# Block-quantised weights prepared inside the first attention, and a low-rank term folded into the K and V weights

## The chip, the cores and the metric

The kernel runs on one core of one Trainium2 chip. The metric is the device time of one execution in microseconds (us). A core has five engines with a queue of instructions each: TensorE (PE in the profile, PEld for its weight loads), VectorE (DVE), ScalarE (ACT), GpSimd (POOL) and SyncE (SP, which here issues DMAs). They meet only at semaphores. The profile gives TensorE's granted clock as a share of 2.4 GHz: 1.00 is that, 0.50 is 1.2 GHz.

## The reference

Two layers over x of 4 x 1024 tokens by 256, with a context of 4 x 64 tokens by 192. Each layer is attention and then an MLP, both on a layer norm with a residual. The parts that the change touches are the weights of layer 0's MLP and the K and V of layer 1's attention:

```python
def lpbq_dequant(w):                       # w_gate, w_up: 768 x 256, w_down: 256 x 768
    O, I = w.shape
    qmax = 2.0 ** (W_BITS - 1) - 1.0       # W_BITS = 4, BLOCK = 32
    wb = w.reshape(O, I // BLOCK, BLOCK)
    s = jnp.maximum(jnp.max(jnp.abs(wb), axis=-1, keepdims=True) / qmax, 1e-12)
    wq = jnp.clip(jnp.round(wb / s), -qmax - 1.0, qmax) * s
    return wq.reshape(O, I)
...
x = act_qdq(x)                             # one scale over the whole normed x
up = act_qdq(x @ lpbq_dequant(w_up).T)
gate = act_qdq(x @ lpbq_dequant(w_gate).T)
sig = fixed_qdq_u16(jax.nn.sigmoid(gate))
gate = act_qdq(gate * sig)
o = act_qdq(gate * up)
return o @ lpbq_dequant(w_down).T
...
k_in = org_ctx @ Wk + _lora(org_ctx, k_down, k_up, k_alpha)   # rank 32, first 60 tokens
v_in = org_ctx @ Wv + _lora(org_ctx, v_down, v_up, v_alpha)
ipa_k = ipa_ctx @ Wk_ipa                                      # last 4 tokens
ipa_v = ipa_ctx @ Wv_ipa
```

## The kernel before

Everything lives in SBUF from stage to stage, and the stages follow one another as blocks: every engine waits at the end of a block until all have arrived. The 4096 tokens are 32 tiles of 128 (`NT`), tile t in `x_res[:, t, :]`. Matrices that TensorE multiplies are split in two f16 parts (`hi`, `lo`), which makes three products of each. The order of the work is written out by hand: each engine has its own loop, and there is no planner.

**Attention, layer 0** (`attention`, line 680). Each engine runs the same steps k over the tiles, with different tiles in flight, through `in_steps_by`: the first and last steps are written out, those between are a hardware loop of four steps (`Fori`). VectorE's step (line 961) is: `residual(k-2)`, `sums(k+1)`, `statistics(k-2)`, `inverses(k+1)`, `maxima(k+3)`, `rest_x(k+4)`, `rest_p(k)`. TensorE's is `scores(k+3)`, `turn_x(k+4)`, `turn_probs(k)`, `output(k-1)`. `scores(k+4)` needs what `rest_x(k+4)` writes. GpSimd's step is `normalise(k+1)`, which starts when `inverses(k+1)` has written `ri`, then `subtract(k+3)`, which needs `mx` of `maxima(k+3)`, then `add_bias(k+4)`; all three read and write SBUF (line 996 for the first two).

**Between attention and the MLP.** SyncE clears the semaphores (`clear_semaphores`, line 95). `quantise_weights` (line 1025) loads the three MLP weights (768 KB each) into `qw_w`, 128 x 1536 each; for each of them VectorE runs a chain in which every instruction waits for the one before: block maxima (L1068), their maximum (L1069), scale (L1070), its reciprocal (L1071), multiply (L1072), round (L1073), clip (L1074), multiply back (L1075). Then five small instructions make the powers of two `un` and `up` (L1077 to L1081), and the weights are turned on TensorE (L1117), four 128 x 128 blocks to a bank, nine banks, and split by ScalarE (`high`, L1095) and VectorE (`low`, L1086). `rstd_of` (line 642) turns the statistics into `rstd` and `nmr` (L652 to L666). `quantise_input` (line 1122) norms four tiles at a time (eight groups; ScalarE L1140), takes their largest value (L1159), turns them (L1151) and copies them into `xT` (L1164); it ends with the scale of the whole x. `gated_mlp` starts then: its first matmul (L1233) needs the scaled xT.

**gated_mlp** (line 1184) has three blocks. "gu" makes gate (16 units) and then up (16 units of 128 x 1536, `NU`), and SyncE stores up in HBM (L1395). "go" multiplies gate by up in 16 units: SyncE loads up again (L1426), ScalarE makes integer levels (L1506, L1508), VectorE multiplies and takes a maximum (L1520, L1514). Beside this, TensorE makes layer 1's K and V, 16 tiles of 128 x 256 (8 of K, 8 of V): SyncE loads the low-rank factors (`low_in`, eight DMAs), Wk and Wk_ipa, and, behind the third up load, Wv and Wv_ipa, into `xq`, which is free in this block. TensorE makes the two rank-32 products `cd` of the context (L1455), then for each tile two matmuls of Wk or Wv over 60 tokens of each batch (L1469, 128 and 64 rows), one of the low-rank factor (L1471, 32 rows) and two of the ipa weights over 4 tokens (L1474). ScalarE copies the tiles back (`keep`, L1488), one or two in each of the units 4 to 14 before the unit's own work; the six banks make a ring. "gd" is the down projection (from L1566).

The arena of 24576 floats per partition is taken after layer 0's attention: gate, xT, and later layer 1's `M` lie in it.

## Time and profile before

| | us |
|---|---|
| median of 3 runs (1607.9 to 1612.33) | 1609.33 |
| the profiled execution | 1618.78 |
| its span, first to last instruction | 1616.9 |
| PE busy / DVE busy / ACT busy / POOL busy | 1322.4 / 1037.8 / 809.5 / 518.5 |
| layer 0's attention, steady steps | 137 to 309 |
| last work of that attention to first matmul of the MLP | 326.4 to 395.7 |
| go, first K matmul to last copy | 572.5 to 642.3 |

An engine's busy time is the sum of its instructions' spans; a number after an arrow says what the engine had waited for. For this kernel the busy shares say little, since its stages have different limits: in attention TensorE has no gap, between attention and MLP VectorE works alone, and in go TensorE has no gap again, at half its clock.

### The profile page before, as it was taken

To read this page: it belongs to the slowest core of one execution; us is meant where nothing else is said; L and a number is where in the kernel's file an instruction comes from. 1 tells how busy PE (TensorE), PEld (TensorE's weight loads), DVE (VectorE), ACT (ScalarE), POOL (GpSimd) and SP (SyncE) were. 2 spreads that over 40 slices of the span, in tenths; PEclk is the share of its full clock that TensorE was granted. 3 is DMA by queue.
4 is the path that set the end of the run, shared out by engine and by line. 5 is a ranking of instruction groups with operands and counts; after the bars stand their busy time and mean duration, and the time that the engine had idled before them with its cause. 6 is when DMAs were issued, how large, how long until landed. Compare 5 with 4: busy or idle time off the path is not lost. (4 is left out here: it accounts for less than half of the span.)

```text
span 1616.9 us, 29377 instructions
## 1 busy us (share of the span) xinstructions
PE 1322.4 (82%) x8855; PEld 976.9 (60%) x8856; DVE 1037.8 (64%) x1908; ACT 809.5 (50%) x1173; POOL 518.5 (32%) x427
## 2 busy tenths in 40 slices
PE   5968999925997398598879999664099999999996
PEld 2435777713433145485546666564089989989995
DVE  2866777777569865464758888755255665666553
ACT  0345665505479665642567777564043344344341
POOL 1016777600000000001066767437513333333233
PEclk9979999957999755795899999855599999999998
DMA  5000000010013374200012122275422222222221
GB/s 199 1 3 1 1 0 0 1 59 1 0 66 148 143 235 169 106 8 1 11 46 93 63 90 65 59 276 173 151 54 45 47 49 40 46 47 51 40 44 12
DMA packets 63211, 106.86 MB, mean 66 GB/s; under 512 B 9712, under 2 KB 50768, under 8 KB 62000
## 3 DMA queue, kind: packets, MB, share of 16 engines
q1 hardware_dynamic: 48848, 89.17, 16.4%
q0 software_dynamic: 14304, 16.93, 5.7%
q8 instruction: 33, 0.54, 0.1%
q14 instruction: 26, 0.21, 0.0%
HBM read 67.89 MB, written 40.01 MB: 67 GB/s over the span
## 5 line engine op out<-in xcount | busy, mean ns | idle before, releaser
L2154 POOL DMA_INDIRECT out<-ex_yo,ex_mt x78 | 135.0, 1731 | 315.6 <-DVE ex_yo L2129 181.2
L2031 PE MATMUL ex_ps_h<-ex_xT_hi,a_arena 128*128 128x256 f16 x1248 | 211.8, 274 | 0.0
L2073 ACT ACTIVATE ex_hT<-ex_ps_h,e_b1T,e_unscale 128x256 f32<-128x256 f32 x312 | 150.5, 562 | 114.7 <-PE ex_ps_h L2031 114.7
L794 PE MATMUL at_ps_y<-c_VW,at_pT_hi 128*128 (+1 forms) x1024 | 171.9, 273 | 1.3 <-DVE main_x_res L921 1.3
L2031 PE MATMUL ex_ps_h<-ex_xT_lo,a_arena 128*128 128x256 f16 x624 | 170.7, 274 | 0.0
L2044 PE MATMUL ex_ps_y<-e_w_lo,ex_hT_hi 128*128 x624 | 170.2, 273 | 0.0
L2044 PE MATMUL ex_ps_y<-a_arena,ex_hT_lo 128*128 x624 | 170.2, 273 | 0.0
L2044 PE MATMUL ex_ps_y<-a_arena,ex_hT_hi 128*128 x624 | 170.2, 273 | 0.0
L996 POOL TENSOR_TENSOR at_sc<-at_sc,at_ri 128x960 f32<-128x960 f32 (+1 forms) x96 | 127.3, 1340 | 87.0 <-DVE at_ri L916 86.7
L1233 PE MATMUL gm_bank<-f_xq,f_wide 128*128 (+1 forms) x576 | 128.8, 384 | 21.2 <-ACT gm_stg L1271 16.2
L996 POOL TENSOR_TENSOR at_sc<-at_sc,at_mx 128x960 f32<-128x960 f32 (+1 forms) x96 | 127.2, 1339 | 43.1 <-DVE at_mx L893 42.9
L794 PE MATMUL at_ps_y<-c_VW,at_pT_lo 128*128 (+1 forms) x512 | 139.9, 273 | 0.0
L893 DVE TENSOR_REDUCE at_mx<-at_sc 128x16 f32<-128x960 f32 (+1 forms) x96 | 79.1, 852 | 92.3 <-ACT at_sc L829 92.3
L829 ACT COPY at_sc<-at_ps_s 128x1024 f32<-128x1024 f32 x64 | 64.7, 1011 | 134.6 <-PE at_ps_s L772 134.6
L2031 PEld LDWEIGHTS ex_ps_h<-ex_xT_hi,a_arena 128*128 x1248 | 122.5, 98 | 14.5 <-issue 0.3
L1233 PEld LDWEIGHTS gm_bank<-f_xq,f_wide 128*128 128x128 f16 x576 | 55.7, 99 | 94.2 <-issue 17.4
L2064 ACT ACTIVATE ex_xT_hi<-ex_ps_t 128x512 f16<-128x512 f32 x39 | 23.3, 597 | 176.2 <-PE ex_ps_t L2017 176.2
L794 PEld LDWEIGHTS at_ps_y<-c_VW,at_pT_hi 128*128 128x128 f16 x1024 | 100.3, 98 | 13.0 <-issue 1.8
L2105 DVE SCALAR_TENSOR_TENSOR ex_xT_lo<-ex_ps_t,ex_xT_hi 128x512 f16<-128x512 f32 x39 | 27.0, 691 | 113.8 <-ACT ex_xT_hi L2064 113.8
L2115 DVE TENSOR_TENSOR ex_hT_lo<-ex_hT,ex_hT_hi 128x1024 f16<-128x1024 f32 x78 | 95.7, 1227 | 2.7
L772 PE MATMUL at_ps_s<-a_arena,at_xnT_hi 128*128 (+1 forms) x256 | 79.7, 395 | 14.6 <-issue 10.9
L772 PE MATMUL at_ps_s<-c_M,at_xnT_hi 128*128 (+1 forms) x256 | 81.7, 403 | 10.3 <-issue 6.7
(320 smaller groups left out, 2941.7 us busy)
## 6 DMA issues: line engine op xcount, KB each, us to landing
at_half<-in_L_ffn_W SPq DMA_DIRECT2D x32, 512.0 KB, 4.0
up_scratch<-gm_stg SPq DMA_DIRECT2D x16, 768.0 KB, 3.2
gm_stg<-up_scratch SPq DMA_DIRECT2D x16, 768.0 KB, 4.2
ex_row<-xs SPq DMA_DIRECT2D x39, 260.0 KB, 2.7
rt_stage<-in_L_ffn_W SPq DMA_DIRECT2D x16, 512.0 KB, 6.2
main_x_res<-in_x SPq DMA_DIRECT2D x8, 512.0 KB, 12.0
out<-main_x_res SPq DMA_DIRECT2D x4, 1024.0 KB, 11.7
xs<-rt_pad SPq DMA_DIRECT2D x18, 130.0 KB, 2.2
```

Source lines behind the costliest of these rows:

```text
L772: last = nc.tensor.matmul(ps_s[j][:, c * CH:(c + 1) * CH], a[:, d, :], b[:, d, bass.ds(off + c * CH, CH)], start=(n == 0), stop=(n == 3 * ...
L794: last = nc.tensor.matmul(ps_y[:, 0:D], a[j][:, n, :], b[:, bass.ds(off + n * D, D)], start=(n == 0 and i == 0), stop=(n == NP - 1 and i = ...
L829: nc.scalar.copy(sc[j][:, :, :], ps_s[j % 2][:, :].rearrange("p (h k) -> p h k", h=H)).then_inc(ev_r, 1)
L893: last = nc.vector.tensor_reduce(mx[:, j, :, g], sc[j][:, :, lo:hi], AX.X, ALU.max)
L996: last = nc.gpsimd.tensor_tensor(part, part, what[:, j, :, g].unsqueeze(2).to_broadcast([P, H, hi - lo]), op)
L1233: last = nc.tensor.matmul(ps[:, o, :], a[:, d, o * P:(o + 1) * P], b[:, d, bass.ds(c0, CH)], start=(n == 0), stop=(n == 3 * DT - 1))
L2031: last = nc.tensor.matmul(ps_h[:, n, :], a[:, bass.ds(e * WN + d * HID + n * P, P)], b[:, d, :], start=(m == 0), stop=(m == 3 * DT - 1))
L2044: last = nc.tensor.matmul(ps_y[j][:, q, :], a[:, n, q * P:(q + 1) * P], b[:, bass.ds(e * WN + n * D, D)], start=(n == 0 and m == 0), stop= ...
L2073: last = nc.scalar.activation(hT[:, n, :], ps_h[:, n, :], ACT.Relu, bias=b1T[:, bass.ds(e * HT + n, 1)], scale=unscale[:, 0, bass.ds(e, 1)])
L2105: nc.vector.scalar_tensor_tensor(out=xT_lo[j][:, :, :], in0=ps_t[:, :, :], scalar=XN_SCALE, in1=xT_hi[j][:, :, :], op0=ALU.mult, op1=ALU.s ...
L2115: nc.vector.tensor_tensor(hT_lo[j][:, part, :], hT[:, part, :], hT_hi[j][:, part, :], ALU.subtract).then_inc(hlo_r, 1)
L2154: nc.gpsimd.indirect_dma_start(out=acc[:, :], out_offset=bass.IndirectOffsetOnAxis(ap=mt[j][:, q, 1:2].bitcast(U32), axis=0), in_=yo[j][:, ...
```

## The change

Two edits that don't touch each other.

**First edit: the MLP weights.** `quantise_weights` and the `rstd_of` ahead of the MLP are gone. The arena is taken before layer 0's attention, whose `M`, projection weights and `WqT` now lie in it, and so do the three MLP weights. SyncE issues their loads at the start of attention. VectorE does the chain in 12 steps of attention (k = 4 to 15), four for each weight, between `inverses` and `maxima`; for this its loop is written out in full instead of `Fori`. The maximum over partitions is one GpSimd instruction at the end, and the powers follow VectorE's last step. The turning and splitting of the nine banks, and the work of `rstd_of`, go into `quantise_input`.

**Second edit: layer 1's K and V.** The rank-32 up factor is loaded as rows 64 to 95 of the second half of Wk or Wv, and `cd` is put under the context's second half in `ctxe`, so that the low-rank matmul joins the 64-row one (now 96 rows). The down factors are padded with 64 zero columns by GpSimd so that `cd` comes out in rows 64 to 95. The small loads are issued in gu behind its first store, Wk's loads at gu's end, Wv's at go's start; ScalarE does its part of `cd` ahead of unit 0 instead of in units 1 and 2.

```diff
@@ attention, VectorE
+            def levels(i, part):
+                wi, per, am, sc, rs = qw[i], [P, NB, QB], bam[:, i, :], bsc[:, i, :], brs[:, i, :]
+                if part == 0:
+                    dve.wait_ge(loaded[i], 16)
+                    nc.vector.tensor_reduce(am, wi, AX.X, ALU.max, apply_absolute_value=True).then_inc(qc, 1)
+                elif part == 1:
+                    dve.wait_ge(qc, 7 * i + 1)
+                    nc.vector.tensor_reduce(top[:, i:i + 1], am, AX.X, ALU.max).then_inc(top_r, 1)
+                    nc.vector.tensor_scalar(sc, am, 1.0 / 7.0, 1e-12, ALU.mult, ALU.max).then_inc(qc, 1)
...
+                    nc.vector.reciprocal(rs, sc).then_inc(qc, 1)
...
+                    nc.vector.tensor_tensor(wi, wi, rs.unsqueeze(2).to_broadcast(per), ALU.mult).then_inc(qc, 1)
+                elif part == 2:
...
+                    nc.vector.tensor_scalar(wi, wi, MAGIC, MAGIC, ALU.add, ALU.subtract).then_inc(qc, 1)
...
+                    nc.vector.tensor_scalar(wi, wi, 7.0, -8.0, ALU.min, ALU.max).then_inc(qc, 1)
+                else:
...
+                    nc.vector.tensor_tensor(wi, wi, sc.unsqueeze(2).to_broadcast(per), ALU.mult).then_inc(qc, 1)
...
                 if there(k + 1, NT):
                     inverses(k + 1, (j + 1) % NS)
+                if quant and 4 <= k < 16:
+                    levels((k - 4) // 4, (k - 4) % 4)
                 if there(k + 3, NT):
                     maxima(k + 3, (j + 3) % NS)
...
-            in_steps_by(nc.vector, NT, 4, 2, NS, step)
+            if quant:
+                for k in range(-4, NT + 2):
+                    step(k, k % NS)
+                powers()
+            else:
+                in_steps_by(nc.vector, NT, 4, 2, NS, step)
@@ quantise_input, ScalarE
+            high(0)
+            high(1)
+            act.wait_ge(ve_r, 1)
+            nc.scalar.activation(sd[:, :], ve[:, :], ACT.Sqrt).then_inc(sd_r, 1)
+            high(2)
+            act.wait_ge(nmr_r, 1)
+            for g in range(NC):
+                norm(g)
+                if g + 3 < NM:
+                    high(g + 3)
@@ gated_mlp, gu, SyncE
                     sp.dma_start(up_dram[u, :, :], stg[u % 2][:, :]).then_inc(u_st[u % 2], 16)
+                    if u == 0:
+                        sp.wait_ge(u_mm, 1)
+                        for i, n in enumerate("kv"):
+                            split(sp, downs[:, i, :, C1:UP], l1[f"{n}_down"], low_in)
+                            sp.dma_start(alpha[:, i:i + 1], l1[f"{n}_alpha"].unsqueeze(0).to_broadcast([P, 1])
+                                         ).then_inc(low_in, 16)
+                load_kv(sp, 0)
@@ gated_mlp, go, TensorE
-                        for t in range(2):
-                            nc.tensor.matmul(tokens(out, 0, KV - IPA), wt[0:rows[t], t, at],
-                                             tokens(ctxT[0:rows[t], t, :], 0, KV - IPA), start=(t == 0), stop=False)
-                        nc.tensor.matmul(tokens(out, 0, KV - IPA), ups[i][:, at], tokens(cd[i], 0, KV - IPA),
+                        nc.tensor.matmul(tokens(out, 0, KV - IPA), wt[:, 0, at], tokens(ctxT[:, 0, :], 0, KV - IPA),
+                                         start=True, stop=False)
+                        nc.tensor.matmul(tokens(out, 0, KV - IPA), wt[0:UP, 1, at], tokens(ctxe[0:UP, i, :], 0, KV - IPA),
                                          start=False, stop=True)
```

Where the instructions stand. VectorE in layer 0's attention, one step of the loop before, from `sums` on (`at_sm` are the sums, `at_ri` the inverses, `at_mx` the maxima, `at_xnT_lo` what the next scores wait for; the REGISTER and ISA rows are the loop's addresses):

```order
L911 TENSOR_REDUCE at_sm<-at_sc 128x16
L926 ISA
L926 BN_STATS main_stats<-main_x_res 128x6
L916 RECIPROCAL at_ri<-at_sm 128x16
L893 TENSOR_REDUCE at_mx<-at_sc 128x16
L897 REGISTER_ALU
L898 SCALAR_TENSOR_TENSOR at_xnT_lo<-at_ps_xT,at_xnT_hi 128x256
```

and the same place in the changed kernel, in step 5 (the second quarter of the first weight; `at_bam`, `at_bsc`, `at_brs` are block maxima, scales and reciprocals, `a_arena` here the weight):

```order
L847 TENSOR_REDUCE at_sm<-at_sc 128x16
L862 BN_STATS main_stats<-main_x_res 128x6
L852 RECIPROCAL at_ri<-at_sm 128x16
L905 TENSOR_REDUCE at_top<-at_bam 128x1
L906 TENSOR_SCALAR at_bsc<-at_bam 128x48
L908 RECIPROCAL at_brs<-at_bsc 128x48
L910 TENSOR_TENSOR a_arena<-a_arena,at_brs 128x1536
L829 TENSOR_REDUCE at_mx<-at_sc 128x16
L834 SCALAR_TENSOR_TENSOR at_xnT_lo<-at_ps_xT,at_xnT_hi 128x256
```

Four instructions of the weights now stand between the inverses and the maxima, ahead of everything that the next scores wait for; in step 4 it is one (L902), in step 6 two (L913, L915), in step 7 one (L918), and then again for the next weight.

VectorE in the changed kernel at the start of `quantise_input` (`f_wide` receives the low parts of the gate and up weights, `qx_xn` is a group of normed tiles, `qx_ps` the turned one):

```order
L1112 BN_AGGR main_mv<-main_stats 128x2 x32
L1115 TENSOR_SCALAR qx_ve<-main_mv 128x32
L1099 SCALAR_TENSOR_TENSOR f_wide<-qx_ring,a_up,f_wide 128x2x256 x2
L1119 RECIPROCAL main_rstd<-qx_sd 128x32
L1121 SCALAR_TENSOR_TENSOR main_nmr<-main_mv,main_rstd 128x32
L1099 SCALAR_TENSOR_TENSOR f_wide<-qx_ring,a_up,f_wide 128x2x256
L1104 TENSOR_REDUCE qx_am<-qx_xn 128x1
L1099 SCALAR_TENSOR_TENSOR f_wide<-qx_ring,a_up,f_wide 128x2x256
L1104 TENSOR_REDUCE qx_am<-qx_xn 128x1
L1109 COPY a_arena<-qx_ps 128x2x512
```

Before, the nine low parts were all done ahead of the statistics; now three stand ahead of the first group and six among the groups.

TensorE at the start of go, before (`f_xq` holds Wk or Wv and the ipa weights, `f_wide` the low-rank operands):

```order
L1455 MATMUL gm_bank<-main_ctxT,f_wide 32x4x60 x4
L1469 MATMUL gm_bank<-main_ctxT,f_xq 128x4x60 x2
L1471 MATMUL gm_bank<-f_wide 128x4x60
L1474 MATMUL gm_bank<-main_ctxT,f_xq 128x4x4 x2
L1469 MATMUL gm_bank<-main_ctxT,f_xq 128x4x60 x2
```

and now:

```order
L1430 MATMUL gm_bank<-main_ctxT,f_wide 96x4x60 x4
L1441 MATMUL gm_bank<-main_ctxT,f_xq 128x4x60
L1443 MATMUL gm_bank<-f_wide,f_xq 128x4x60
L1446 MATMUL gm_bank<-main_ctxT,f_xq 128x4x4 x2
L1441 MATMUL gm_bank<-main_ctxT,f_xq 128x4x60
```

A tile has four matmuls instead of five: the one over `f_wide` alone is gone, and the second one over the weights reads its moving side from `f_wide`.

## Rows read from the trace of the kernel before

**Rows 1.** By stretch: length, busy PE, PEld, DVE, ACT, POOL, then PEclk, DMA, GB/s.

```profile
137.00:326.00 189.00, 187.08 (x1394) 140.17 (x1392) 142.21 (x239) 109.25 (x172) 128.61 (x85) 1.00 0.00 0
572.00:642.00 70.00, 69.53 (x160) 39.70 (x160) 42.92 (x26) 40.38 (x39) 0.00 (x0) 0.50 0.53 180
835.00:1035.00 200.00, 188.31 (x1364) 138.11 (x1363) 165.35 (x346) 155.67 (x249) 139.42 (x146) 0.99 0.25 77
```

**Rows 2.** Timeline of DVE, one attention step: start, length, what; idle before it.

```profile
216.44 0.48 DVE L921 SCALAR_TENSOR_TENSOR main_x_res<-at_ps_y,c_unscale,main_x_res 128x256 f32 x1
...
218.31 0.23 DVE L916 RECIPROCAL at_ri<-at_sm 128x16 f32<-128x16 f32 x1
220.04 1.22 DVE L893 TENSOR_REDUCE at_mx<-at_sc 128x16 f32<-128x1024 f32 x1 [1.50 <-ACT at_sc L829]
221.18 0.41 DVE L898 SCALAR_TENSOR_TENSOR at_xnT_lo<-at_ps_xT,at_xnT_hi 128x256 f16<-128x256 f32 x1
...
222.75 0.48 DVE L921 SCALAR_TENSOR_TENSOR main_x_res<-at_ps_y,c_unscale,main_x_res 128x256 f32 x1
```

**Rows 3.** Timeline of POOL in the same step.

```profile
218.62 1.90 POOL L996 TENSOR_TENSOR at_sc<-at_sc,at_ri 128x1024 f32<-128x1024 f32 x1 [0.99 <-DVE at_ri L916]
```

**Rows 4.** Timeline of PE in the same step: the scores that need at_xnT_lo.

```profile
222.43 0.59 PE L772 MATMUL at_ps_s<-c_M,at_xnT_hi 128*128 x2
```

**Rows 5.** Timeline from the end of attention to the first MLP matmul.

```profile
325.98 0.43 DVE L926 BATCH_NORM_STATS2 main_stats<-main_x_res 128x6 f32<-128x256 f32 x1
...
329.94 0.38 SPq L1052 DMA_DIRECT2D qw_w<-in_L_ffn_w_gate  x1
...
334.78 1.75 DVE L1068 TENSOR_REDUCE qw_am<-qw_w 128x48 f32<-128x1536 f32 x1 [8.38 <-DMA qw_w<-in_L_ffn_w_gate]
336.57 0.20 DVE L1069 TENSOR_REDUCE qw_top<-qw_am 128x1 f32<-128x48 f32 x1
...
339.18 0.96 DVE L1073 TENSOR_SCALAR qw_w<-qw_w 128x1536 f32<-128x1536 f32 x1
...
341.17 1.76 DVE L1075 TENSOR_TENSOR qw_w<-qw_w,qw_sc 128x1536 f32<-128x1536 f32 x1
...
358.96 0.16 DVE L1077 TENSOR_SCALAR qw_gtop<-qw_gtop 128x3 f32<-128x3 f32 x1
...
360.62 4.29 DVE L1086 SCALAR_TENSOR_TENSOR f_wide<-qw_ring,qw_up,f_wide 128x512 f16<-128x512 f32 x6 [0.81 <-ACT f_wide L1095]
...
367.75 1.28 ACT L666 ACT_TABLE_LOAD   x1 [1.07 <-PEq L78]
367.78 2.21 DVE L652 BATCH_NORM_AGGREGATE main_mv<-main_stats 128x2 f32<-128x6 f32 x32 [0.32 <-PEq L78]
...
371.37 8.18 ACT L1140 ACTIVATE qx_xn<-main_x_res,main_nmr,main_rstd 128x256 f32<-128x256 f32 x16 [0.89 <-PEq L78]
...
395.72 4.62 PE L1233 MATMUL gm_bank<-f_xq,f_wide 128*128 128x512 f16 x11 [4.99 <-DVE f_xq L1312]
```

**Rows 6.** Timeline at the start of layer 1's preparation: two instructions side by side.

```profile
737.01 3.51 POOL L446 MEMSET a_arena<- 128x4096 f32 x1 [82.20 <-POOLq L97]
...
737.05 3.49 DVE L514 TENSOR_SCALAR pa_alpha_r<-a_arena 128x2 f32<-128x2 f32 x1 [4.86 <-PEq L97]
```

**Rows 7.** Timeline of go: first matmuls, one K tile, and the last copy.

```profile
559.06 1.57 ACT L1506 ACTIVATE gm_gq<-a_arena,gm_sc 128x1536 int16<-128x1536 f32 x1 [8.65 <-PEq L78]
...
567.49 3.81 PE L1455 MATMUL gm_bank<-main_ctxT,f_wide 128*32 128x240 f32 x8 [26.79 <-DMA f_wide<-in_L_xattn_v_up]
...
572.47 2.26 PE L1469 MATMUL gm_bank<-main_ctxT,f_xq 128*128 128x240 f32 x4 [1.16 <-DMA f_xq<-in_L_xattn_Wk_ipa]
...
574.66 1.16 PE L1471 MATMUL gm_bank<-f_wide 32*128 32x240 f32 x2
...
576.83 2.26 PE L1469 MATMUL gm_bank<-main_ctxT,f_xq 128*128 128x240 f32 x4
...
642.34 0.37 ACT L1488 COPY f_xq<-gm_bank 128x256 f32<-128x256 f32 x1 [3.99 <-PE gm_bank L1474]
```

More of the change, by code:

```diff
@@ L278, in _ @@
                 last.then_inc(made, 1)
-            for base, ipa in ((wk, wki if lora else None), (wv, wvi if lora else None)):
-                if base is wv and not lora:
+            for base in (wk, wv):
+                if base is wv:
                     pe.wait_ge(late, 16 * len(second))
@@ L1122, in quantise_input @@
[L1122 to L1135 removed]
+                nc.scalar.activation(hi, banked(m), ACT.Copy, scale=up[:, i:i + 1]).then_inc(high_r, 1)
@@ L1136, in _, with norm @@
+            def norm(g):
                 need(act, t_r, g - 1)
@@ L1142, in _, with turn_w, turn_x @@
                 last.then_inc(xn_r, 1)
+            high(0)
[8 more added lines that the diff above has]
+                    high(g + 3)
+            for m in range(NC + 3, NM):
+                high(m)
         @block.tensor
         def _(pe):
-            for g in range(NC):
+            def turn_w(m):
+                i, g = divmod(m, 3)
+                src = w[i].rearrange("p (o b) q -> p o (b q)", o=DT if i == 2 else FT)
+                need(pe, moved, m - 3)
+                for a in range(2):
+                    for b in range(2):
+                        if i < 2:
+                            blk = src[:, 2 * g + b, a * P:(a + 1) * P]
+                        else:
+                            blk = src[:, b, (2 * g + a) * P:(2 * g + a + 1) * P]
+                        last = nc.tensor.transpose(ring[:, m % 4, (2 * a + b) * P:(2 * a + b + 1) * P], blk, ident[:, :])
+                last.then_inc(made, 1)
+            def turn_x(g):
                 pe.wait_ge(xn_r, g + 1)
@@ L1387, in _ @@
                 nc.gpsimd.partition_all_reduce(allr[:, 0:1], red[:, 0:1], P, RMAX).then_inc(gall, 1)
+                pool.wait_ge(u_mm, 1)
+                nc.gpsimd.memset(downs[:, :, :, 0:C1], 0.0).then_inc(low_set, 1)
+                for i in range(2):
+                    nc.gpsimd.tensor_copy(ctxe[0:C1, i, :], ctxT[0:C1, 1, :]).then_inc(low_set, 1)
                 pool.wait_ge(gred, 2)
```

355 lines of the change are left out of this document (133 added, 222 removed).

## The prediction

> **What bounds the kernel now.** I read three views in this order. The busy time by stretch tells which engine has no gap: in layer 0's attention TensorE is busy for 187.1 of 189 us at granted clock 1.00 while VectorE has 142.2, and in go's stretch with the K and V tiles TensorE is busy for 69.5 of 70 us at 0.50 while VectorE has 42.9 and ScalarE 40.4 [rows 1]. The timeline of one attention step then shows where VectorE's spare time lies: a step is 222.75 - 216.44 = 6.31 us, and its one wait, 1.50 us, is between the inverses (done at 218.54) and the maxima at 220.04 [rows 2]. Last, the timeline between attention and MLP shows a chain on VectorE with TensorE idle: from the last statistics, 326.41, to the first MLP matmul, 395.72, 69.3 us pass [rows 5]. So the first edit moves work from a stretch in which nothing hides it into a gap of an engine that isn't the bound, and the second takes a matmul from the bound of its stretch.
>
> **First edit, what goes.** After it the stretch from 326.41 on is made of these. The clearing of the semaphores and the block change stay, 329.94 - 326.41 = 3.5 us [rows 5]; six semaphores more are cleared here and six fewer at the next clearing, so that cancels. The five small powers now end attention: 358.96 to 359.81 (the low at 360.62 less its idle of 0.81), so 0.85 us, exposed as before [rows 5]. Until the first normed tile, ScalarE does two highs (some 0.8 us each, by the idle of 0.81 ahead of the first low), the table load of 1.28 and the root; the statistics of 2.21 us run beside this on VectorE. With about 1.1 us for the first turned bank that is 4.0 us, and 371.37 - 369.99 = 1.4 us lie between statistics and first norm as before, with part of a third high 5.9 us [rows 5]. From the first norm to the first MLP matmul it was 395.72 - 371.37 = 24.35 us, set by VectorE with its maximum and copy for each group; six lows at 4.29 / 6 = 0.715 us now stand among them, 4.3 us, and ScalarE's highs stay under VectorE's time: 28.6 us [rows 5]. The sum is 3.5 + 0.85 + 5.9 + 28.6 = 38.9 us, against 69.3: **30.4 us less**. The loads of the weights (waited for until 334.78) and both chains' block changes are gone with this; the loads run under attention, whose DMA share is 0.00 [rows 1].
>
> **First edit, what attention pays.** The chain costs, by start to start, 1.79 us in its first quarter, 339.18 - 336.57 = 2.61 in its second, 341.17 - 339.18 = 1.99 in its third and 1.76 in its last [rows 5]. It stands in the gap of 1.50, so the maxima start later by 0.29, 1.11, 0.49 and 0.26, that is 2.15 us for a weight and 6.5 for three. VectorE is the bound for these 12 steps, and queued behind each piece are the maxima and at_xnT_lo, for which TensorE's scores wait; they start 222.43 - 221.59 = 0.84 us after it [rows 2, 4], a slack that is used up once: 5.6 us. That is the lower end.
>
> But the gap is not empty on the neighbour: GpSimd's normalise starts at 218.62, right behind the inverses, and lasts to 220.52 [rows 3]. In this trace a tensor_scalar from SBUF to SBUF of two elements a partition took 3.49 us, and ended with the GpSimd memset of 3.51 us that had started 0.04 us before it [rows 6]. I take it that such an instruction waits for the GpSimd one that is running, and the other way round. In the second quarter L906 (the tensor_scalar) comes behind the small L905, so behind normalise's start: it is held until 220.52, and 2.4 us are then left, so the maxima start at 222.9, 2.9 us late. In the third the first tensor_scalar is ahead of normalise (VectorE's next instruction starts 0.08 us before its last one ends), normalise goes between the two (1.90), and the second comes behind: 0.99 + 1.90 + 1.0 from 218.46 on, 2.3 us late. The first quarter is a reduce and the last one starts ahead: 0.29 and 0.26. Together 5.75 for a weight, 17.3 for three, less the slack: **16.4 us more**, the value I take, since the held instruction is of the same kind. If normalise gets ahead in the last quarter too, that adds 1.9 three times: 22 us, the upper end. GpSimd's delay of some 2 us costs nothing, as the probabilities are wanted a whole step later.
>
> The Trainium skill (SBUF — State Buffer, Who interferes with whom) states this as a rule: VectorE and GpSimd share one pair of ports, held for a whole instruction by whichever starts first, and both tensor_scalar from SBUF and an instruction with two SBUF inputs need it, a reduce does not. The memset row agrees for the tensor_scalar. No row here shows the two-input case held. By the rule the sum is the 16.4 us above; by the plain durations it would be 5.6 us.
>
> **Second edit.** A K tile took 576.83 - 572.47 = 4.36 us, and its two wide matmuls 2.19, so 1.09 each [rows 7]. The low-rank one, of the same width, goes: 3.27 us. The 96-row matmul is taken at the price of the 64-row one, since those of 128 and 64 rows are in the same 2.19; the clock stays at 0.50, as in the whole stretch [rows 1]. TensorE stood waiting for the small loads until 567.49 though the block had begun at 559.06; it can start at once now, since the small loads come in gu and Wk's behind gu's last store, under VectorE's tail. The start until the first tile, 572.47 - 567.49 = 5.0 us, gets 0.3 for the wider products: first tile at 564.4, last one done at 564.4 + 16 x 3.27 = 616.7, where it was 642.3 [rows 7]: 25.5 us less. ScalarE starts its unit 0 some 5 us later, which doesn't show as long as a unit takes less than (616.7 - 564.4) / 14 = 3.7 us; the 42.9 and 40.4 us of VectorE and ScalarE in that stretch [rows 1] fit in 52.3. What follows the last copy stays. In gu, GpSimd's padding and copies (three instructions of at most 256 elements a partition, each between 0 and the 1.9 us of a 1024-element one [rows 3]) may hold VectorE: 0.5 us. Six small DMA issues ahead of gu's second store have a whole unit of time. **25.0 us less.**
>
> **Sum.** -30.4 + 16.4 - 25.0 = -39.0 us. The profiled execution of 1618.78 us would become 1579.8; it is 9.4 us above the median of the runs shown, 1609.33, and the terms don't depend on that, so the median becomes **1570.3 us**.
>
> **The rivals.** (1) No holding by GpSimd: attention pays 5.6 us, the sum is -49.8, 1559.5 us. For it: no row shows VectorE's large instructions held. Against it: the 3.49 us of two elements. (2) Normalise gets ahead in every quarter but the first: 22 us, the sum is -33.4, 1576. (3) In go the units, not the tiles, set the end: it decides from 3.7 us a unit; at the 4.36 us of today's tiles the last unit is some 9 us later, 1579. Against it are the busy times. (4) In go TensorE gets the full clock, since its work is denser without the low-rank matmul: the units set the end some 5 us earlier, 1565. Against it: the stretch was gapless and stayed at 0.50. (5) Slower: the gaps of up to 2.9 us that VectorE now makes in TensorE's work let the granted clock fall to 0.50 in the 12 steps. A step of 6.31 us of gapless work then takes another 6.31, 75.7 us in all, against the 30.4 + 25.0 = 55.4 that the edits bring: +20 us, 1629.6; it decides from 55.4 / 6.31 = 8.8 steps at the lower clock. Against it: layer 1's attention leaves TensorE idle for 11.7 of 200 us with a clock of 0.99 [rows 1].
>
> **How the numbers follow.** Forecast 0.56, rival 1 0.20, rival 2 0.08, rival 3 0.05, rival 4 0.04, rival 5 0.04, and 0.03 that terms fail together and leave it where it is. Both signs: 0.93 is faster by over 0.3% (4.8 us, about what runs of this kernel tell apart), 0.03 within it, 0.04 slower. The range reaches from rival 1 with 3 us for the spread of the runs to rival 3: 1556 to 1581.
>
> **What would show it.** After the last statistics the first MLP matmul comes about 39 us later. In attention the steps k = 4 to 15 come in fours: near 6.5, 9.2, 8.6 and 6.5 us if GpSimd holds, 6.6, 7.4, 6.8, 6.6 if not; L906 then lasts near 2 us instead of 0.2, and the second tensor_scalar of the third quarter near 2.9 instead of 0.96. The granted clock there stays at 1.00. In go the K tiles start within 6 us of the block at 3.27 us each. The prediction is wrong if the small pieces in attention push the scores by more than their own length plus one normalise, or if ScalarE waits for up loads rather than for tiles in go.

## The result and the profile after

The changed kernel takes **1561.33 us** (median of 3 runs, 1559.65 to 1561.85) where the kernel before took 1609.33. The ratio is 0.970, with a 95% interval of 0.967 to 0.972, so 48.0 us less. The prediction was 1570.3 us with a range of 1556 to 1581: right in sign and range, 9 us too high.

The profiled execution took 1561.33 us, with a span of 1559.6. Against the profiled one of before, 1618.78, it is 57.4 us less, and that is 9.4 us more than the medians differ. Points at which the work passes from stage to stage, from both timelines, tell where the difference lies:

| stage | before | after | change | predicted |
|---|---|---|---|---|
| start to the first turned tile of attention 0 | 103.3 | 91.1 | -12.2 | 0 |
| attention 0: first turned tile to the start of the last statistics | 222.7 | 233.4 | +10.7 | +16.4 |
| from there to the first MLP matmul | 69.7 | 38.4 | -31.3 | -30.4 |
| MLP, first to last matmul of gu | 144.6 | 144.9 | +0.3 | +0.5 |
| last matmul of gu to first of gd | 126.1 | 97.2 | -28.9 | -25.5 |
| all that follows, to the end of the span | 950.5 | 954.6 | +4.1 | 0 |

The first row is no effect of the change, as experiment 1 shows.

By stretch (length, busy PE, PEld, DVE, ACT, POOL, then PEclk, DMA, GB/s), which answers to [rows 1]. The first is layer 0's attention: TensorE now has 12.5 us of idle time, at the full clock, and VectorE is busy for 20 us more. The second is go, at the lower clock.

```profile
137.00:326.00 189.00, 176.53 (x1305) 131.33 (x1303) 161.84 (x254) 101.83 (x160) 126.05 (x80) 1.00 0.00 0
...
526.00:596.00 70.00, 47.24 (x136) 39.11 (x136) 54.98 (x40) 53.85 (x52) 0.35 (x1) 0.50 0.70 234
```

**The stretch behind attention** is as predicted. One timeline of all engines (start, length, engine, line, what, count, and in brackets the idle time before it), which answers to [rows 5]:

```profile
324.53 0.43 DVE L862 BATCH_NORM_STATS2 main_stats<-main_x_res 128x6 f32<-128x256 f32 x1
...
325.54 0.17 DVE L932 TENSOR_SCALAR a_up<-a_up 128x3 f32<-128x3 f32 x1
...
329.76 2.22 DVE L1112 BATCH_NORM_AGGREGATE main_mv<-main_stats 128x2 f32<-128x6 f32 x32 [4.05 <-PEq L97]
...
334.62 2.08 ACT L1046 ACTIVATE qx_xn<-main_x_res,main_nmr,main_rstd 128x256 f32<-128x256 f32 x4
...
362.88 1.46 PE L1217 MATMUL gm_bank<-f_xq,f_wide 128*128 128x512 f16 x3 [4.55 <-DVE f_xq L1296]
```

The reader is to see four steps from the end of the statistics at 324.96: the powers until 325.71, clearing and block change until 329.76, until the first norm 334.62 - 329.76 = 4.9 us, and from it to the first matmul 362.88 - 334.62 = 28.3 us.

**Attention** pays. The timelines of DVE and of POOL, which answer to [rows 2, 3]; a "piece" is one of the four parts of a weight's chain. First a step with the second piece, then one with the third and one with the last. The rows of L857 are the residuals, so from one to the next is a step:

```profile
176.57 0.48 DVE L857 SCALAR_TENSOR_TENSOR main_x_res<-at_ps_y,c_unscale,main_x_res 128x256 f32<-128x256 f32 x1
...
178.64 0.18 DVE L906 TENSOR_SCALAR at_bsc<-at_bam 128x48 f32<-128x48 f32 x1
178.85 0.45 DVE L908 RECIPROCAL at_brs<-at_bsc 128x48 f32<-128x48 f32 x1
179.34 2.92 DVE L910 TENSOR_TENSOR a_arena<-a_arena,at_brs 128x1536 f32<-128x1536 f32 x1
182.19 1.21 DVE L829 TENSOR_REDUCE at_mx<-at_sc 128x16 f32<-128x1024 f32 x1
...
184.84 0.47 DVE L857 SCALAR_TENSOR_TENSOR main_x_res<-at_ps_y,c_unscale,main_x_res 128x256 f32<-128x256 f32 x1
```

```profile
178.75 1.90 POOL L976 TENSOR_TENSOR at_sc<-at_sc,at_ri 128x1024 f32<-128x1024 f32 x1 [0.94 <-DVE at_ri L852]
```

```profile
156.02 0.47 DVE L857 SCALAR_TENSOR_TENSOR main_x_res<-at_ps_y,c_unscale,main_x_res 128x256 f32<-128x256 f32 x1
...
158.02 0.90 DVE L913 TENSOR_SCALAR a_arena<-a_arena 128x1536 f32<-128x1536 f32 x1
158.95 2.53 DVE L915 TENSOR_SCALAR a_arena<-a_arena 128x1536 f32<-128x1536 f32 x1
...
164.06 0.47 DVE L857 SCALAR_TENSOR_TENSOR main_x_res<-at_ps_y,c_unscale,main_x_res 128x256 f32<-128x256 f32 x1
...
166.06 1.69 DVE L918 TENSOR_TENSOR a_arena<-a_arena,at_bsc 128x1536 f32<-128x1536 f32 x1
...
170.32 0.48 DVE L857 SCALAR_TENSOR_TENSOR main_x_res<-at_ps_y,c_unscale,main_x_res 128x256 f32<-128x256 f32 x1
```

```profile
158.18 2.49 POOL L976 TENSOR_TENSOR at_sc<-at_sc,at_ri 128x1024 f32<-128x1024 f32 x1 [0.94 <-DVE at_ri L852]
...
166.22 3.29 POOL L976 TENSOR_TENSOR at_sc<-at_sc,at_ri 128x1024 f32<-128x1024 f32 x1 [0.94 <-DVE at_ri L852]
...
172.49 1.90 POOL L976 TENSOR_TENSOR at_sc<-at_sc,at_ri 128x1024 f32<-128x1024 f32 x1 [0.43 <-DVE at_ri L852]
```

The rows read as if whoever starts first kept the other waiting, and experiment 3 tests that. The product L910 started 0.59 us after GpSimd's normalise and took 2.92 us, where the same instruction took 1.76 in the kernel before with GpSimd idle. It ends 1.6 us after normalise, which ends at 180.65. In the third piece L913 was ahead, normalise (2.49 us for 1.90) waited for its end, and L915 (2.53 us for 0.96) waited for normalise. In the last piece the product was ahead and took its plain length, and normalise stretched to 3.29. At 172.49 VectorE runs the first piece, a reduce of 1.70 us over 1536 elements, and normalise keeps its 1.90. The steps of the first, second, third and last piece took 6.25, 8.27, 8.04 and 6.26 us, where a step without a piece takes 6.31.

**go**, which answers to [rows 7], in the timelines of PE, ACT and DVE:

```profile
526.65 4.21 PE L1430 MATMUL gm_bank<-main_ctxT,f_wide 128*96 128x240 f32 x8 [18.52 <-PEq L78]
...
531.40 1.17 PE L1441 MATMUL gm_bank<-main_ctxT,f_xq 128*128 128x240 f32 x2 [0.54 <-ACT f_wide L1454]
532.37 1.01 PE L1443 MATMUL gm_bank<-f_wide,f_xq 96*128 96x240 f32 x2
533.16 0.98 PE L1446 MATMUL gm_bank<-main_ctxT,f_xq 128*128 128x16 f32 x4
534.08 1.17 PE L1441 MATMUL gm_bank<-main_ctxT,f_xq 128*128 128x240 f32 x2
...
574.63 0.98 PE L1446 MATMUL gm_bank<-main_ctxT,f_xq 128*128 128x16 f32 x4
```

```profile
542.74 1.58 ACT L1479 ACTIVATE gm_sq<-gm_stg,gm_sc 128x1536 int16<-128x1536 f32 x1 [3.91 <-DMA gm_stg<-up_scratch]
...
580.33 0.69 ACT L1460 COPY f_xq<-gm_bank 128x256 f32<-128x256 f32 x2
```

```profile
544.42 1.76 DVE L1491 TENSOR_TENSOR a_arena<-gm_gq,gm_sq 128x1536 f32<-128x1536 int16 x1 [3.53 <-ACT gm_sq L1479]
546.09 1.75 DVE L1485 TENSOR_REDUCE gm_pmax<-a_arena 128x1 f32<-128x1536 f32 x1
547.75 1.75 DVE L1491 TENSOR_TENSOR a_arena<-gm_gq,gm_sq 128x1536 f32<-128x1536 int16 x1
...
592.80 0.17 DVE L1496 TENSOR_REDUCE gm_red<-gm_pmax 128x1 f32<-128x16 f32 x1
```

The first tile starts 4.9 us after the block, and a tile takes 534.08 - 531.40 = 2.68 us, not 3.27. The tiles end at 575.6, 17.2 us before the unit work does at 592.80. In the kernel before that distance was 11.9 us, from 642.3 to this row of its DVE timeline:

```profile
654.19 0.17 DVE L1525 TENSOR_REDUCE gm_red<-gm_pmax 128x1 f32<-128x16 f32 x1
```

From 544.42 on VectorE has no gap, at 547.75 - 544.42 = 3.33 us a unit. So the units and not the tiles set the end, and they were held by a load, 3.91 us ahead of 542.74. The prediction had named just this, ScalarE waiting for up loads rather than for tiles, as a sign that it is wrong.

### The profile page after: what moved, and what is told of

The parts are those of the page before. It is cut to its first block and busy times, and to the rows that moved or that the text cites. A ratio compares the mean times of both kernels' runs of the same rounds, so it can differ in the third digit from the quotient of the medians.

```text
span 1559.6 us, 29136 instructions
## 1 busy us (share of the span) xinstructions
PE 1280.5 (82%) x8823; PEld 967.2 (62%) x8824; DVE 1042.2 (67%) x1908; ACT 809.1 (52%) x1173; POOL 522.7 (34%) x430
## 3 DMA queue, kind: packets, MB, share of 16 engines
q1 hardware_dynamic: 48848, 89.17, 17.2%
## 5 line engine op out<-in xcount | busy, mean ns | idle before, releaser
L708 PE MATMUL at_ps_s<-a_arena,at_xnT_hi 128*128 (+1 forms) x512 | 162.8, 401 | 34.0 <-issue 26.7
L976 POOL TENSOR_TENSOR at_sc<-at_sc,at_ri 128x960 f32<-128x960 f32 (+1 forms) x96 | 133.4, 1403 | 83.5 <-DVE at_ri L852 83.2
L708 PEld LDWEIGHTS at_ps_s<-a_arena,at_xnT_hi 128*128 128x128 f16 x512 | 51.3, 101 | 93.4 <-issue 48.9
L730 PEld LDWEIGHTS at_ps_y<-c_VW,at_pT_hi 128*128 128x128 f16 x1024 | 100.0, 98 | 12.7 <-issue 1.8
L708 PE MATMUL at_ps_s<-a_arena,at_xnT_lo 128*128 (+1 forms) x256 | 102.1, 399 | 0.0
## 6 DMA issues: line engine op xcount, KB each, us to landing
main_x_res<-in_x SPq DMA_DIRECT2D x8, 512.0 KB, 11.9
```

Of the source, the lines that this page charges most:

```text
L708: last = nc.tensor.matmul(ps_s[j][:, c * CH:(c + 1) * CH], a[:, d, :], b[:, d, bass.ds(off + c * CH, CH)], start=(n == 0), stop=(n == 3 * ...
L730: last = nc.tensor.matmul(ps_y[:, 0:D], a[j][:, n, :], b[:, bass.ds(off + n * D, D)], start=(n == 0 and i == 0), stop=(n == NP - 1 and i = ...
L976: last = nc.gpsimd.tensor_tensor(part, part, what[:, j, :, g].unsqueeze(2).to_broadcast([P, H, hi - lo]), op)
```

## The experiments

All runs were timed against the kernel before on their own chip, and chips differ: its median was 1622.4 us in the first set, 1605.9 in the second and 1623.9 in the third. Most of that lies in layer 1's MLP, which sends every token to some of several expert weights: from the last tile turned for the choice of experts (the route) to the first one turned for the experts' products 45.9 to 47.8 us pass in the profiles of the first measurement and of the second set, and 53.7 to 58.9 in those of the first and third set, whatever the kernel. So kernels of different sets are compared by stages, from the timelines (attention 0 from the first turned tile to the start of the last statistics, then to the first MLP matmul, then from gu's last matmul to gd's first):

| kernel | set | median | attention 0 | to first MLP matmul | gu's last to gd's first |
|---|---|---|---|---|---|
| token axis flat | 1 | 1623.9 | 220.0 | 69.8 | 126.3 |
| second edit alone | 1 | 1589.7 | 222.9 | 69.8 | 96.6 |
| first edit alone | 1 | 1602.5 | 233.3 | 38.4 | 127.1 |
| pieces ahead of inverses | 1 | 1563.0 | 225.4 | 38.4 | 96.7 |
| changed kernel | 2 | 1561.6 | 233.5 | 38.3 | 96.9 |
| units 2, 3 ahead of Wv | 2 | 1560.4 | 233.1 | 38.4 | 97.9 |
| loads not early | 2 | 1569.5 | 232.5 | 38.4 | 108.1 |
| 27 pieces, units ahead | 2 | 1548.9 | 222.4 | 38.3 | 98.6 |
| changed kernel | 3 | 1575.9 | 233.2 | 38.4 | 97.0 |
| Wv loaded in gu | 3 | 1572.7 | 232.9 | 38.4 | 94.0 |
| third product | 3 | 1586.8 | 233.4 | 38.3 | 112.9 |
| 27 pieces, Wv in gu | 3 | 1561.7 | 222.1 | 38.4 | 95.6 |

The 220.0 in the first line, where the kernel before has 222.7, is no cheaper step: the steps take the same time as before, and the difference lies ahead of the first residual.

**1. The 12.2 us ahead of attention.** The diff also writes layer 0's K and V projections with a flat token axis, and the prediction had no term for that. The edit, made in the kernel before:

```diff
-                            last = nc.tensor.matmul(
-                                ring[:, b, 0:B * KV].rearrange("p (b k) -> p b k", b=B)[:, :, lo:hi],
-                                wt[0:m, t, j * P:(j + 1) * P],
-                                ctxT[0:m, t, :].rearrange("p (b k) -> p b k", b=B)[:, :, lo:hi],
-                                start=(t == 0), stop=(t == 1))
+                            last = nc.tensor.matmul(ring[:, b, 0:B * KV], wt[0:m, t, j * P:(j + 1) * P], ctxT[0:m, t, :],
+                                                    start=(t == 0), stop=(t == 1))
```

> The kernel before with one edit: the K and V projections of layer 0 write and read their 256 tokens as one flat axis and not as 4 groups of 64 (the diff changes this on the side, and my prediction has no term for it). In the profiles the 64 matmul records of these projections stand 0.575 us apart before and 0.314 after the change, and the first score-matrix product starts at 59.84 and 47.26 us. Theory A, the access pattern is the cause: the projections take 0.31 us a record here too, the stage ends some 12.6 us earlier, and the median is 1609.3 - 12.6 = 1596.7 us. Theory B, the profiled execution of the kernel before ran its projections at the lower clock by chance (it was 9.4 us above its median): the median stays within 3 us of 1609.3.

Its time over that of before is 1.002 (0.998 to 1.006): no gain. The matmuls of Wk in the timelines of PE, in the kernel before and in the kernel with the second edit alone, which keeps the old axis:

```profile
22.18 18.31 PE L288 MATMUL pa_ring<-main_ctxT,pa_wk 128*128 128x256 f32 x32
```

```profile
22.52 10.01 PE L288 MATMUL pa_ring<-main_ctxT,pa_wk 128*128 128x256 f32 x32
```

The same code took 18.3 us once and 10.0 us once. The first score-matrix product came at 59.8 us in that one profile and between 46.5 and 48.6 in the thirteen others. Only one of the thirteen, the second edit alone, has the old token axis; that the axis brings nothing is shown by the medians above.

The clock tells what happened in that execution. In go at clock 0.50 the median weight load takes 310 ns, and so it does here, where the kernel with the second edit alone shows 186. The row of the clock prints 1.00 for the stretch, but the trace of before holds no record of the clock ahead of 65.4 us, and a stretch without one prints as 1.00. The timeline of PEld shows the change at that record, within one run of equal weight loads:

```profile
65.12 0.34 PEld L298 LDWEIGHTS pa_ring<-pa_Kd,pa_WqT 128*128 128x128 f32 x1 [0.52 <-issue]
65.72 0.19 PEld L298 LDWEIGHTS pa_ring<-pa_Kd,pa_WqT 128*128 128x128 f32 x1 [0.26 <-issue]
```

In the thirteen other traces the first record of the clock stands between 21.5 and 25.1 us, and the weight loads shorten there too. So theory B holds with its mechanism: TensorE ran this stage at the lower clock until 65.4 us, some 40 us longer than in the others, after the same start. Its 1618.78 us are 9.4 above the median of that kernel, and the late stage is 12.2. Why the clock rose late that once is open. Without the 12.2 us the profiled pair differs by 45.1 us, and the medians by 48.0 (and by 1605.9 - 1561.6 = 44.3 in the second set).

**2. Each edit alone.** The gated MLP of one kernel put into the other.

> The kernel before with the second edit alone (the low-rank product folded into 96 rows, small loads and Wk's in gu). My prediction's term is -25.0, which gives 1584.3 us; the profile of the changed kernel, read from the last gated matmul to the first down matmul, gives -28.9, which gives 1580.4. In either case layer 0's attention and the 69 us after it are as in the kernel before. If the edits only bring their sum together, this and the first edit alone add up to -48.0.

> The changed kernel with the gated MLP of the kernel before, so the first edit alone (with the flat token axis). My prediction's terms are -30.4 + 16.4 = -14.0, which gives 1595.3 us. The profile of the changed kernel gives -31.4 for the stretch after attention and +10.7 for attention, -20.7, which gives 1588.6; if the flat token axis brings 12.6 in every execution and not in the profiled one alone, it is 1576.

The ratios to before are 0.980 (0.975 to 0.984) and 0.987 (0.982 to 0.991), by the medians -32.7 and -19.9 us, together -52.6 against -48.0; on this chip the runs of before spread over 23 us, so the stages tell more. Each edit acts in its own stages: go's way is shorter with the second alone (96.6 us, against 97.2 with both), and attention is longer and the stretch behind it shorter with the first alone (233.3 and 38.4, against 233.4 and 38.4). The edits add up.

**3. Is it GpSimd that makes the pieces long?** VectorE's step, with `levels` moved:

```diff
+                if quant and 4 <= k < 16:
+                    levels((k - 4) // 4, (k - 4) % 4)
                 if there(k + 1, NT):
                     inverses(k + 1, (j + 1) % NS)
-                if quant and 4 <= k < 16:
-                    levels((k - 4) // 4, (k - 4) % 4)
```

> The changed kernel with each piece of the weights' chain put ahead of the inverses, where GpSimd waits for VectorE and nothing of it runs. Theory A, the pieces cost more than their length because GpSimd's normalise runs beside them (2.92 us for the first product where 1.76 is its length, 2.53 for the second tensor_scalar where 0.90 is): none is held here, the steps with the second and third piece go from 8.27 and 8.04 us to about 7.1 and 6.35, which is 2.9 us for a weight and 8 us for three: 1561.3 - 8 = 1553 us. Theory B, VectorE reads its operands more slowly in these forms whatever GpSimd does: the durations stay at 2.9 and 2.5 us and the time at 1561. Rival C, normalise now starts up to 2.5 us later and the subtract behind it too, so the exponentials come late and the gain is given back: the time is 1558 or more though the durations fall.

The timelines of DVE and of POOL there:

```profile
147.90 0.47 DVE L857 SCALAR_TENSOR_TENSOR main_x_res<-at_ps_y,c_unscale,main_x_res 128x256 f32<-128x256 f32 x1
...
150.55 1.76 DVE L910 TENSOR_TENSOR a_arena<-a_arena,at_brs 128x1536 f32<-128x1536 f32 x1
152.22 0.25 DVE L852 RECIPROCAL at_ri<-at_sm 128x16 f32<-128x16 f32 x1
...
154.99 0.47 DVE L857 SCALAR_TENSOR_TENSOR main_x_res<-at_ps_y,c_unscale,main_x_res 128x256 f32<-128x256 f32 x1
...
156.84 0.98 DVE L913 TENSOR_SCALAR a_arena<-a_arena 128x1536 f32<-128x1536 f32 x1
157.85 0.96 DVE L915 TENSOR_SCALAR a_arena<-a_arena 128x1536 f32<-128x1536 f32 x1
...
161.49 0.47 DVE L857 SCALAR_TENSOR_TENSOR main_x_res<-at_ps_y,c_unscale,main_x_res 128x256 f32<-128x256 f32 x1
```

```profile
152.55 1.90 POOL L976 TENSOR_TENSOR at_sc<-at_sc,at_ri 128x1024 f32<-128x1024 f32 x1 [2.75 <-DVE at_ri L852]
```

Theory A. No operand and no shape was changed, only GpSimd's product no longer stands beside them, and L910 falls from 2.92 to 1.76 us, L915 from 2.53 to 0.96. Attention takes 225.4 us, 8.0 less, as expected. The steps with the second and third piece take 154.99 - 147.90 = 7.09 and 161.49 - 154.99 = 6.50 us. That is what VectorE's own work of 4.55 us (6.25 less the reduce of 1.70) and the pieces' 2.5 and 2.0 us add up to, so the later normalise cost nothing and rival C falls. The time by itself can't show the 8 us: the median of 1563.0 us is from the first set, in which the changed kernel did not run. Its ratio to before, 0.962 (0.958 to 0.967), lies below the changed kernel's 0.970 to 0.973.

The Trainium skill (SBUF — State Buffer, Who interferes with whom) states this as an exclusive lock that whoever starts first holds for its whole instruction. By it a VectorE instruction with two SBUF inputs needs the lock against a GpSimd one that reads SBUF, a tensor_scalar needs it in its 2-port mode, and a reduce never does. The three cases here, 2.92 us, 2.53 us and the reduce beside a normalise of 1.90, agree.

**4. The changed kernel again**, for the second and third set.

> The changed kernel itself once more, on the same chip as the other runs of this set, so that they can be compared with it. The time is 1561 us where the kernel before has 1609; on another chip both may be later by the same amount. Layer 0's preparation is expected as in the first profile of the changed kernel (first score-matrix product near 47.3 us), since two of three kernels with the old token axis had it there too.

> The changed kernel on the chip of this set, as the one to compare with: 1561 us where the kernel before has 1606 to 1609.

1561.6 and 1575.9 us, with ratios to before of 0.973 (0.970 to 0.976) and 0.972 (0.967 to 0.976), as in the first measurement.

**5. The early start alone and the fold alone.** Without the early loads: six small loads out of gu's queue and Wk's too, all issued in go.

```diff
                 load(0)
                 load(1)
+                for i, n in enumerate("kv"):
+                    split(sp, downs[:, i, :, C1:UP], l1[f"{n}_down"], low_in)
...
+                load_kv(sp, 0)
+                load(2)
                 load_kv(sp, 1)
-                load(2)
```

> The changed kernel with the small loads and Wk's issued in go, as in the kernel before, and not in gu: the fold alone. In the kernel before TensorE waited until 567.49 for the small loads, 8.4 us after the block began, and ScalarE's unit 0 did not wait for them. Here the low-rank copies stand ahead of unit 0, so the units start some 8 us later too: go is 8 us longer and the time 8 us above the changed kernel's. If the units ran under the loads as before it is 0 to 3 us. My prediction's term for the early start was 564.4 against 572.5 for the first tile, so 8.1 us of the 25.0.

go's way is 11.2 us longer (108.1 for 96.9) and the median 7.9 us higher, where 8 was expected. Counted from gu's last matmul ScalarE's unit 0 starts 8.0 us later. The rest of the 11.2 is a load again: Wk's and Wv's loads now stand ahead of unit 3's, and ScalarE waits 7.10 us for it, where in the changed kernel of this set it waits 3.53 for unit 2's (timeline of ACT):

```profile
556.21 1.57 ACT L1477 ACTIVATE gm_sq<-gm_stg,gm_sc 128x1536 int16<-128x1536 f32 x1 [7.10 <-DMA gm_stg<-up_scratch]
```

And without the cheaper tile, with the early start:

```diff
                         nc.tensor.matmul(tokens(out, 0, KV - IPA), wt[0:UP, 1, at], tokens(ctxe[0:UP, i, :], 0, KV - IPA),
-                                         start=False, stop=True)
+                                         start=False, stop=False)
+                        nc.tensor.matmul(tokens(out, 0, KV - IPA), wt[C1:UP, 1, at], tokens(ctxe[C1:UP, i, :], 0, KV - IPA),
+                                         start=False, stop=True)
```

> The changed kernel with a third wide product in each K/V tile, over the 32 low-rank rows once more, so that the low-rank term stands twice in layer 1's keys and values: the tile of the kernel before with the early start of the changed one. A wide product took 0.8 to 1.1 us, so a tile goes from 2.67 to about 3.6, and the last one ends near 531.4 + 16 * 3.6 = 589 us on the scale of the changed kernel, 15 us later than there. Theory A, the units set go's end at 3.33 us each: ScalarE waits only for the last copies, 0 to 6 us in all. Theory B, the tiles set it, as my prediction took it: 14 us or more.

go's way is 112.9 us against 97.0, 15.9 more. The waits in it (engine, who waited, for what; us in all, times, longest), and the first tile in the timeline of PE:

```profile
ACT f_xq L1462 <- PE gm_bank L1448: 15.3, 9, 3.7
```

```profile
532.30 1.17 PE L1441 MATMUL gm_bank<-main_ctxT,f_xq 128*128 128x240 f32 x2 [0.54 <-ACT f_wide L1456]
533.27 1.01 PE L1443 MATMUL gm_bank<-f_wide,f_xq 96*128 96x240 f32 x2
534.20 1.16 PE L1445 MATMUL gm_bank<-f_wide,f_xq 32*128 32x240 f32 x2
535.30 1.15 PE L1448 MATMUL gm_bank<-main_ctxT,f_xq 128*128 128x16 f32 x4
536.37 1.17 PE L1441 MATMUL gm_bank<-main_ctxT,f_xq 128*128 128x240 f32 x2
```

Theory B: with this tile the tiles set the end again, and ScalarE waits 15.3 us for them. My estimate of the tile was wrong: it is 536.37 - 532.30 = 4.07 us, not 3.6. The third product takes 1.10 by itself, and its neighbours are longer beside it, the 96-row one 0.93 for 0.79 and the four small ones 1.07 for 0.92. So adding a product of 32 rows costs 1.4 us here, not 1.1.

This tile is not yet the old one, which took 4.36 us. Its last part stands in the timeline of PE of the kernel before:

```profile
575.75 1.15 PE L1474 MATMUL gm_bank<-main_ctxT,f_xq 128*128 128x16 f32 x4
```

With [rows 7], from start to start, the old tile is 2.19 us for the products of 128 and 64 rows, 1.09 for the one of 32 rows and 1.08 for the four small ones. The new one is 1.76 for the products of 128 and 96 rows and 0.92 for the small ones. So 1.09 of the 1.68 us saved are the product that is gone, 0.43 are the two wide ones and 0.16 the small ones. Fold 15.9 and early start 11.2 are 27.1 of the 28.9 us.

**6. Do the units set go's end now?** First the loads of units 2 and 3 ahead of Wv's.

```diff
                 load(0)
                 load(1)
+                load(2)
+                load(3)
                 load_kv(sp, 1)
-                load(2)
-                for u in range(3, NU):
+                for u in range(4, NU):
```

> The changed kernel with one edit in go: the loads of units 2 and 3 are issued ahead of those of Wv, not behind them. In the profile of the changed kernel ScalarE stands 3.91 us waiting for unit 2's load, and from 544.42 us on VectorE works without a gap at 3.33 us a unit until the last maximum, 18 us after the last K/V tile. Theory A, the units set go's end: the time falls by 3.9 us against the changed kernel. Theory B, the tiles and their copies set it: nothing falls. Rival C, ScalarE then waits for a V tile, since Wv comes later: less than 2 us is left.

The time is that of theory B, but by another cause: the wait only moved, from unit 2 to unit 4 (timeline of ACT).


```profile
549.75 1.57 ACT L1480 ACTIVATE gm_sq<-gm_stg,gm_sc 128x1536 int16<-128x1536 f32 x1 [4.76 <-DMA gm_stg<-up_scratch]
```

The unit whose load stands behind Wv's 1.66 MB waits for them. The median is 1560.4 us against 1561.6, no difference. So next Wv's loads went under VectorE's tail in gu:

```diff
                 load_kv(sp, 0)
+                load_kv(sp, 1)
...
                 load(1)
-                load_kv(sp, 1)
                 load(2)
```

> The changed kernel with Wv's five loads issued behind Wk's in gu, and none of them in go. With units 2 and 3 loaded ahead of Wv the wait did not go, it moved: ScalarE stood 4.76 us for unit 4's load in place of 3.91 for unit 2's, since the load behind Wv's 1.66 MB waits for them wherever that is. Theory A, Wv's bytes delay a unit by about 4 us and the units set go's end: with these bytes moved under VectorE's tail in gu, where the queue is empty from 522 us on, the last maximum comes 4 us earlier and the time falls by 4 against the changed kernel. Theory B, the queue is full there too and the first unit's load comes late: ScalarE waits for unit 0, and less than 1.5 us is left. Theory C, the tiles set the end: nothing falls.

go's way is 94.0 us against 97.0, and the longest wait for a load is 0.33 us. Theory A, with 3.0 us of the 4 (the wait that went was 3.62 us in the changed kernel of this set): the units set the end, and a load had delayed them. The medians, 1572.7 and 1575.9, agree but spread too much to show it by themselves.

**7. A better version.** The chain in 27 pieces, the longest 1.14 us (each large instruction in two halves), one in each of the steps k = 2 to 28, ahead of the inverses. The first kernel has it with the load order of experiment 6's first edit, the second with Wv's loads in gu:

```diff
-                if quant and 4 <= k < 16:
-                    levels((k - 4) // 4, (k - 4) % 4)
+                if quant and 2 <= k < 29:
+                    levels((k - 2) // 9, (k - 2) % 9)
```

> The changed kernel with the go edit (units 2 and 3 loaded ahead of Wv) and the weights' chain in 27 pieces of at most 1 us in the steps k = 2 to 28, each ahead of the inverses. With the four pieces a weight ahead of the inverses, layer 0's attention took 225.4 us from its first turn to its last statistics, against 233.4 in the changed kernel and 222.7 in the kernel before. The gap of VectorE is 1.5 us a step, so the pieces fit: attention near 222.8, 10.6 us less than the changed kernel, and with 3.9 us in go 14.5 us less in all. If a piece costs the step even where it is shorter than the gap, attention stays at 225 or more and the gain is 12 or less.

> The chain in 27 pieces ahead of the inverses, and Wv's loads in gu. The pieces brought 12.7 us (1548.9 against 1561.6 on one chip), with attention at 222.4 us. If the loads in gu bring 4 us, this is 16 to 17 us below the changed kernel; if not, 12 to 13.

Attention takes 222.4 and 222.1 us, and a steady step takes 6.29 to 6.39 us, as in the kernel before (6.28 to 6.45): the chain costs nothing. By the busy time of each engine in stretches of attention (length, then busy PE, PEld, DVE, ACT, POOL with the number of instructions, PEclk), first in the changed kernel, then with 27 pieces:

```profile
150.00:220.00 70.00, 61.75 (x450) 45.14 (x447) 69.69 (x93) 38.00 (x60) 46.69 (x28) 1.00 0.00 0
130.00:230.00 100.00, 90.91 (x653) 65.69 (x651) 96.60 (x139) 53.19 (x84) 68.66 (x42) 1.00 0.00 1
```

```profile
130.00:230.00 100.00, 100.00 (x734) 73.94 (x732) 89.09 (x153) 60.75 (x96) 70.78 (x47) 1.00 0.00 1
```

In the changed kernel VectorE has no gap from 150 to 220 us, and TensorE idles for 9 of the 100 us from 130 to 230; with 27 pieces TensorE idles for none. The times are 1548.9 us with a ratio to before of 0.966 (0.963 to 0.968), 12.7 below the changed kernel on the same chip, and in the third set 1561.7 with 0.963 (0.959 to 0.967), 14.2 below it. The first has no gain from go, which is 1.7 us longer there (98.6 for 96.9). Attention gives 11.1, and the 3.3 us by which 12.7 exceeds the sum of the two are within the spread of its runs (1546 to 1560). The second was to gain 4 us in go and got 1.4: ScalarE waited 1.80 us for unit 0's load. Both are faster than the kernel before and than the changed one.

## Why the prediction was right, and where it missed

- **The stretch behind attention, -30.4: right**, measured -31.3. Of its terms the clearing with the powers was 4.8 us for 4.35, the way to the first norm 4.9 for 5.9, and from the norm to the matmul 28.3 for 28.6.
- **Attention, +16.4: right in mechanism, mis-sized**, measured +10.7. The steps with a piece are longer than one without by (-0.06, 1.96, 1.73, -0.05) us, 3.58 for a weight, where the prediction made the maxima later by (0.29, 2.9, 2.3, 0.26), 5.75 for a weight, and took 0.84 off once. Two steps of its working failed. First, "it is held until 220.52", said of L906: it was not held and lasted 0.18 us. It started 0.11 us ahead of normalise, and the reciprocal behind it ran beside normalise in its plain 0.45 us. Only the product was held, from 0.59 us after normalise's start, which is 0.8 us less. Second, the prediction added the excess over the 1.50 gap to a step of 6.31. But VectorE's own work is 4.55 us a step when it has no gap, not 4.81, so each step hides some 0.25 us more, and a piece of 1.70 us hides wholly. The rest is the third piece, 3.46 us long where 3.89 were taken.
- **The second edit, -25.0: right in sign and start, wrong about what sets go's end**, measured -28.6 with gu. The start was 4.9 us for 5.3. Two errors then partly cancelled. The tile took 2.68 us and not 3.27, because the prediction took the 96-row product at the price of the 64-row one and left the others as they were, while experiment 5 shows the wide pair and the small products cheaper too. With 2.68 its own formula gives 564.4 + 16 x 2.68 = 607.3, so 35.0 us less than 642.3. But what it named as a sign of being wrong came true: ScalarE waited for an up load, and the units set the end at 3.33 us each, which gave some 6 us of that back. So the nearness of -25.0 to the measured value is in part luck.
- **"What follows stays"**: nearly, +4.1 us over 950, of which 2.0 in layer 1's attention. That took 239.0 to 239.2 us in three profiles of the changed kernel and 235.8 to 238.9 in the others, those of before among them, and no run separates a cause from the spread.
- **The rivals.** Rival 1 (no holding) gave 1559.5 us, nearest to the time, and its mechanism is refuted: the holding is there at 2.92 and 2.53 us. It is near by luck: its 5.6 us for attention are 5.1 too few, and the 3.6 and 0.9 us that the second edit and the stretch brought beyond the forecast made up for that. Rival 2 fell, since in the last piece VectorE is ahead. Rival 3's mechanism came true without its price: the units set go's end, but at 3.33 us each where it needed 3.7, and the stage is shorter than forecast. Rival 4 and rival 5 fell: the clock is 0.50 in go and 1.00 in attention.
- **The miss.** By its steps the forecast had -39.0; the stages it spoke of gave -49.2, which is 5.7 us from attention, 3.6 from the second edit and 0.9 from the stretch beyond it. Then 4.1 came back later: -45.1, against medians that differ by 48.0.

## What to carry to other kernels

A gap of one engine can be filled without loss by pieces that are shorter than it and that stand where the engine which would hold them up is idle. Here 12 pieces behind the inverses cost 10.7 us, the same 12 ahead of them 2.7, and 27 short ones ahead of them nothing; short ones behind them were not tried. When one edit takes the bound from a stage, look at once for the load that now starts the next bound late. Here moving it behind other loads of the same queue only moved the wait, and moving it out of the stage removed it. And before a difference of two profiles is explained, a stage that the change hardly touches should be compared: one execution may be 12 us late there for no reason in the code. A printed clock of 1.00 at the start of a trace should then be checked against the length of equal instructions.

## What the runs showed of the hardware

- Two f32 products with both inputs in SBUF, one on GpSimd and one on VectorE, did not run side by side, in either order: GpSimd's of 1.90 us stretched to 3.29 behind VectorE's, and VectorE's of 1.76 to 2.92 behind GpSimd's. A VectorE tensor_scalar of 0.96 us stretched to 2.53 in the same way. A reduce over 1536 elements and a reciprocal of 48 ran beside GpSimd's product, and it kept its 1.90 us.
- TensorE ran one execution of fourteen at the lower clock for some 40 us longer than the others: its weight loads fell from 0.34 to 0.19 us at 65.4 us, where the trace has its first record of the clock, and in the others at 21.5 to 25.1 us. It cost 12.2 us.
- Products of fewer rows weren't cheaper: of 240 columns at the lower clock, one of 128 rows took 0.97 us ahead of one of 96 rows, one of 96 rows 0.79, or 0.93 ahead of one of 32 rows, and one of 32 rows 1.09 to 1.10. A pair of 128 and 64 rows took 2.19 us, a pair of 128 and 96 rows 1.76. Why is not shown.
- A stage that writes and reads tokens in HBM took 46 to 48 us in six profiles (those of the first measurement and of the second set) and 54 to 59 in the eight of the two other sets, whatever the kernel.
